# Gated cross-attention block with four rounds of experts: the subtraction of the largest score moved into the exponential

## The reference

```
q   = xn @ Wq.T + bq            # 16 heads of 8 channels
k,v = ctx @ Wkv.T + bkv         # 77 context tokens
att = softmax(q k^T / sqrt(8))  # over the 77 context tokens, per head
x   = x + tanh(g_xattn) * ((att v) @ Wo.T + bo)
x   = x + tanh(g_ffn) * experts(layernorm(x))   # 4 rounds, 4 experts, the 2 best by a router
```

## Time and profile before

| | us |
|---|---|
| median of 3 runs | 538.82 |
| lowest to highest | 538.28 to 539.25 |
| the profiled execution, its own time | 538.98 |
| its span, from the first to the last instruction | 537.2 |

### The profile page before, as it was taken

How to read it: one execution, slowest core, us unless ns; L and a number is a source line. 1 busy time by engine, 2 the same in 40 slices (tenths; PEclk the granted TensorE clock), 3 DMA queues, 4 the chain that set the end, 5 groups by cost and what they waited for, 6 DMA issues and landing times.

```text
span 537.2 us, 8396 instructions
## 1 busy us (share of the span) xinstructions
PE 497.2 (93%) x2529; PEld 402.4 (75%) x2529; DVE 407.7 (76%) x792; ACT 373.1 (69%) x717; POOL 78.7 (15%) x149
## 2 busy tenths in 40 slices
PE   0967998999779999999999999999999999999996
PEld 0945777777567878878888887888788888887884
DVE  3789898889855977697787769768776866876775
ACT  1444556655456887788688778778887877878873
POOL 3374466565300000000000000000000000000000
PEclk9985999999988999999999999999999999999999
DMA  5500000000004012004002100300210040031001
GB/s 135 163 2 0 2 0 0 0 0 0 2 0 159 1 65 94 1 0 159 1 2 83 76 0 1 157 2 0 107 52 1 1 159 0 1 112 67 20 1 39
DMA packets 13063, 22.39 MB, mean 42 GB/s; under 512 B 5200, under 2 KB 9957, under 8 KB 10981
## 3 DMA queue, kind: packets, MB, share of 16 engines
q1 hardware_dynamic: 9648, 21.42, 11.3%
q10 hardware_dynamic: 3381, 0.55, 0.6%
HBM read 20.79 MB, written 1.18 MB: 41 GB/s over the span
## 4 chain that ended last, share of the span: by engine, by line
PE 88%; DVE 6%; ACT 2%; DMA 1%; ACTq 1%; issue 1%; DVEq 0%
PE ps L1121 11%; PE ps L1123 11%; PE ps L1122 11%; PE ps L1101 11%; PE ps L1103 11%; PE ps L1102 11%; PE ps L1015 7%; PE ps L993 4%; PE ps L1002 3%; ACT probT L507 2%; DMA rows_in<-in_L_xattn_bkv_dram 1%; PE ps L949 1%; PE ps L1089 1%; PE ps L1033 1%; DVE v_blk L691 1%
## 5 line engine op out<-in xcount | busy, mean ns | idle before, releaser
L801 DVE TENSOR_TENSOR h_lo<-g_sb,h_hi 128x512 fp32r<-128x512 f32 x256 | 169.8, 687 | 81.2 <-ACT h_hi L597 81.2
L590 ACT ACTIVATE g_sb<-ps,cols 128x512 f32<-128x512 f32 x256 | 175.7, 687 | 75.4 <-PE ps L1103 74.8
L597 ACT ACTIVATE h_hi<-g_sb 128x512 fp32r<-128x512 f32 x256 | 154.1, 631 | 0.0
L1121 PE MATMUL ps<-h_hi,w_hi 128*128 128x512 f32 x256 | 103.5, 404 | 0.0
L1101 PE MATMUL ps<-x_hi,w_hi 128*128 128x512 f32 x256 | 102.2, 399 | 0.8 <-DVE x_lo L795 0.8
L1103 PE MATMUL ps<-x_hi,w_lo 128*128 128x512 f32 x256 | 101.9, 398 | 0.0
L1123 PE MATMUL ps<-h_hi,w_lo 128*128 128x512 f32 x256 | 101.9, 398 | 0.0
L1122 PE MATMUL ps<-h_lo,w_hi 128*128 128x512 f32 x256 | 101.2, 395 | 0.0
L1102 PE MATMUL ps<-x_lo,w_hi 128*128 128x512 f32 x256 | 101.2, 395 | 0.0
L811 DVE SCALAR_TENSOR_TENSOR contrib<-ps,cols,cwb 128x512 f32<-128x512 f32 x64 | 47.8, 746 | 14.0 <-PE ps L1123 8.4
L1101 PEld LDWEIGHTS ps<-x_hi,w_hi 128*128 128x128 f32 x256 | 48.6, 190 | 12.3 <-issue 1.0
(11 more groups left out here) (129 smaller groups left out, 504.1 us busy)
## 6 DMA issues: line engine op xcount, KB each, us to landing
cwb<-cw_rows SPq DMA_DIRECT2D x16, 1024.0 KB, 5.7
x_sb<-in_x_dram SPq DMA_DIRECT2D x4, 256.0 KB, 8.8
w_in<-in_L_ffn_W_dram SPq DMA_DIRECT2D x1, 1024.0 KB, 7.9
out_dram<-xn SPq DMA_DIRECT2D x4, 256.0 KB, 2.3
ctx_sb<-in_ctx_dram ACTq DMA_DIRECT2D x1, 462.0 KB
cw_rows<-cwT SPq DMA_DIRECT2D x8, 16.0 KB, 1.4
wq_in<-in_L_xattn_Wq_dram SPq DMA_DIRECT2D x1, 64.0 KB, 2.7
bv_row<-in_L_xattn_bkv_dram ACTq DMA_DIRECT2D x1, 64.0 KB, 9.1
```

The source lines that it names most:

```text
L590: nc.scalar.activation(g_sb[:, k, :], ps[:, k, :], ACT.Gelu_apprx_tanh, bias=b1_c[:, e * NF + k:e * NF + k + 1]).then_inc(gelu_done, 1)
L597: nc.scalar.activation(h_hi[:, u % 2, k, :], g_sb[:, k, :], ACT.Copy).then_inc(hi_done, 1)
L801: nc.vector.tensor_tensor(h_lo[:, u % 2, k, :], g_sb[:, k, :], h_hi[:, u % 2, k, :].bitcast(F32), ALU.subtract).then_inc(lo_done, 1)
L1121: mm(yb, w2_hi[:, w], hh, start=k == 0, stop=False)
```

## The change

The scores come out of PE negated and scaled: ACT copies Wq's transpose with the factor `-SCALE`, and the bias of q is taken times `-SCALE` too (`bq_s`, a new tile of one column, written by one new ACTIVATE in the start). So the smallest of the negated scores of a head is the negated maximum. DVE takes that minimum (`least`, one tile per parity of b) and subtracts nothing. ACT then computes `exp(-score + least)` straight from PSUM; since the bias is one number per partition and head, this takes one ACTIVATE of 77 columns per head, 8 for each half, in place of one of 616 columns. The tile `shifted` is gone. A score bank may now be written again only once the exponentials have read it: `scores(b+1, half)` waits for `exp_done` of `(b, half)`, and so does the first matmul of the expert stage.

```diff
-        bq_c = cols[:, NCOL - 2:NCOL - 1]
+        bq_s = sb("bq_s", [P, 1])
...
-        mx = sb("mx", [P, H])
+        least = sb("least", [P, 2, H])
...
-        shifted = early("shifted", [P, NQ, HM])
...
-            nc.scalar.activation(wT[:, 0, :], bank(J_W)[:, 0:P], ACT.Copy)
+            nc.scalar.activation(wT[:, 0, :], bank(J_W)[:, 0:P], ACT.Copy, scale=-SCALE)
...
+            nc.scalar.activation(bq_s[:, :], COLS[:, NCOL - 2:NCOL - 1], ACT.Copy, scale=-SCALE)
...
-            def exponentials(b, half, first=False):
-                cols = slice(half * 2 * HM, (half + 1) * 2 * HM)
-                act.wait_ge(sub_done, 2 * b + half + 1)
+            def exponentials(b, s, half, first=False):
+                act.wait_ge(least_done, 2 * b + half + 1)
                 if not first:
                     act.wait_ge(pt_done, NG * b)
                     act.wait_ge(den_done, b)
-                nc.scalar.activation(prob[:, cols], shifted[:, :, :].rearrange("p q n -> p (q n)")[:, cols],
-                                     ACT.Exp, scale=SCALE).then_inc(exp_done, 1)
+                for h in range(2 * HQ * half, 2 * HQ * (half + 1)):
+                    q, k = h // HQ, h % HQ
+                    t = nc.scalar.activation(prob[:, h * M:(h + 1) * M], ps[:, SC + q, k * M:(k + 1) * M],
+                                             ACT.Exp, scale=-1.0, bias=least[:, s, h:h + 1])
+                t.then_inc(exp_done, 1)
...
-                                     ACT.Identity, bias=bq_c[:, 0:1]).then_inc(pre_act, 1)
+                                     ACT.Identity, bias=bq_s[:, 0:1]).then_inc(pre_act, 1)
...
-            def shift(b, half, first=False):
+            def smallest(b, s, half):
 
                 two = slice(2 * half, 2 * half + 2)
                 scores = ps[:, SC + 2 * half:SC + 2 * half + 2, 0:HM].rearrange("p q (h m) -> p q h m", m=M)
                 dve.wait_ge(scores_done, 2 * b + half + 1)
-                nc.vector.tensor_reduce(mx_v[:, two, :], scores, AX.X, ALU.max).then_inc(mx_done, 1)
-                dve.wait_ge(mx_done, 2 * b + half + 1)
-                if not first:
-                    dve.wait_ge(exp_done, 2 * b + half - 1)
-                nc.vector.tensor_tensor(shifted[:, two, :].rearrange("p q (h m) -> p q h m", m=M), scores,
-                                        mx_v[:, two, :].unsqueeze(3).to_broadcast([P, 2, HQ, M]),
-                                        ALU.subtract).then_inc(sub_done, 1)
+                nc.vector.tensor_reduce(least[:, s, :].rearrange("p (q h) -> p q h", q=NQ)[:, two, :], scores, AX.X,
+                                        ALU.min).then_inc(least_done, 1)
...
                 if not first:
-                    pe.wait_ge(sub_done, 2 * b - 1 + half)
+                    pe.wait_ge(exp_done, 2 * b - 1 + half)
...
-            pe.wait_ge(sub_done, 2 * B)
+            pe.wait_ge(exp_done, 2 * B)
```

More of the change, by code:

```diff
@@ L222, in flamingo_gated_block @@
         scores_done = sem("scores_done")
-        mx_done = sem("mx_done")
-        sub_done = sem("sub_done")
+        least_done = sem("least_done")
         exp_done = sem("exp_done")
@@ L551, in attend @@
                 if scores:
-                    exponentials(b + 1, 0)
-                    exponentials(b + 1, 1)
+                    exponentials(b + 1, 1 - s, 0)
+                    exponentials(b + 1, 1 - s, 1)
             assert TC >= 2
@@ L565, in _ @@
             act.wait_ge(moe_ld, 16 * 3)
-            exponentials(0, 0, first=True)
-            exponentials(0, 1, first=True)
+            exponentials(0, 0, 0, first=True)
+            exponentials(0, 0, 1, first=True)
             attend(0, 0, first=True)
@@ L705, in _ @@
                                     ALU.subtract).then_inc(wg_split, 1)
-            mx_v = mx[:, :].rearrange("p (q h) -> p q h", q=NQ)
-            def shift(b, half, first=False):
+            def smallest(b, s, half):
                 two = slice(2 * half, 2 * half + 2)
@@ L747, in attend @@
                 if scores:
-                    shift(b + 1, 0)
+                    smallest(b + 1, 1 - s, 0)
                 if queries:
@@ L753, in attend @@
                 if scores:
-                    shift(b + 1, 1)
+                    smallest(b + 1, 1 - s, 1)
                 if residual:
@@ L761, in _ @@
             dve.wait_ge(xres_step, 2)
-            shift(0, 0, first=True)
-            shift(0, 1, first=True)
+            smallest(0, 0, 0)
+            smallest(0, 0, 1)
             attend(0, 0, values=False, residual=False)
```

## The result

The changed kernel takes 601.84 us (median of 4 runs, 600.19 to 603.5) against 538.55 us: a ratio of 1.1174, 95% interval 1.114 to 1.1208. The forecast was 590.7 us with a range of 568 to 611. The direction and the ring were right; 11 us are missing. The measured time lies in the stretch that the prediction gave to rival C (over 600 us, chance 0.16) and not in that of its own forecast (583 to 600): the clock cost nearly what C said.

What follows compares the result with a forecast made beforehand. PE and DVE were taken as nearly full, PE setting the 5.92 us round. Profiled 538.98 + 36.5 (ring, first and last rounds, start) + 15.4 (clock) = 590.9, median 590.7 us; range 568 to 611.

Steps and rivals of the forecast that it cites:

- the ring: Attention rounds: transposes, moves, widening, eight exponentials, scores, values, transposes close into 8.40 us, from 5.97; +31.6 us over 13 rounds.
- rival C: Attention: clock low for most of each round, recovery late; 606 us at 2.2 us a round, 623 throughout; chance 0.16.
- What bounds the kernel: Attention: PE and DVE nearly full, ACT with room but waiting each iteration for PE's transposes, 29.0 us in all.
- The short exponentials: ACT's 77-column exponentials: 0.33 us each, steps of 0.21, one half 1.80 us, both 3.5 against 1.31 before.
- Rival D: Cheap exponentials at the step's lower end: half 1.05 us, ring 0.75 shorter, 564 us at full clock; chance 0.04.
- The first rounds: Start of attention: first exponentials at about 43.0, later second scores and transposes delay the next scores by 2.7 us.
- The last round: End of attention: `move_rT` behind both halves of the last exponentials delays PE's projection and the attention's end by 2.15 us.
- The sum at the full clock: Whole kernel: 31.6 + 2.7 + 2.15 + 0.1 = +36.5 us; 575.3 us if the clock holds (rival A, chance 0.32).
- The clock: PE's 2.45 us pause each round lowers its clock in most rounds: 1.1 us a round, 15.4 us for 14 rounds.
- The clock behind each wait: Skill's kernel starts each matmul burst cold after a wait; earlier falls agree, but no row showed a pause returning each round.

Runs made afterwards that it cites:

- The run with two buffers: Changed kernel with two buffers for the probabilities, the first half of the exponentials ahead of ACT's moves of the transposed probabilities: 546.64 us.
- the short exponentials alone: Kernel before with 16 exponentials of 77 columns per batch, read from the SBUF copy with a zero bias; subtraction and the scores' wait for it stay: 592.57 us.
- the pause filled: Changed kernel plus 8 unread fp32 matmuls of 128 columns before the first scores of every batch from the third on: 575.11 us.
- the fastest version: Changed kernel with one minimum per query and half, one ACTIVATE per half, two probability buffers and the first half ahead of the moves: 528.62 us.
- its other layout: Kernel before, same instructions, small tiles laid out so the expert stage's tiles lie at the fastest version's addresses: 532.4 us.
- the wait alone: Kernel before with the scores waiting for the exponentials instead of the subtraction; SBUF copy and 616-column exponentials stay: 572.61 us.

## Why the prediction was right, and where it was short

- *What bounds the kernel.* Right: ACT's room could not be used, since its order is tied to PE's transposes. The run with two buffers shows it: the same work in another place of the queue, 546.6 us.
- *The short exponentials.* The step of 0.21 us and the half of 1.80 were measured at 0.21 (3.54 us for 16) and 1.82 to 1.90. Part of that is luck: one operation lasts 0.38 us on the mean, not 0.33, and more than the 0.355 that stood as the upper end, and two of them overlap by 0.17 us, not 0.12. The two errors cancel in the step. Rival D is out.
- *The ring.* 8.40 us worked out, 8.22 measured with the clock held. The ring through the second half and `move_rT` (7.9 us) was not in the prediction as a ring; it was only charged once, for the last round. It didn't change the sum, because it is the shorter one, but it is why the short exponentials alone cost 54 us.
- *The first rounds.* From the first exponentials to exponentials 2 the changed kernel takes 17.85 us (42.05 to 59.90), the one with the pause filled 17.94; 17.7 were worked out (43.0 to 60.7). The length was right. The +2.7 is met only by the latter (60.69 against 57.99); the changed kernel started its first exponentials 0.9 us earlier than forecast, so it is +1.9 there.
- *The last round.* +2.15 worked out; from the start of exponentials 15 to the end of the span the changed kernel takes 405.6 us, before 401.6: +4.0. PE waited 3.54 us for `move_rT` there, and the transposes behind it ran at the low level (2.50 us for ten), which the prediction did not charge.
- *The sum at the full clock.* 575.3 worked out, 575.1 measured with the pause filled. That it is this close is luck: the ring was 0.18 us too long in 13 rounds (2.3 us), and the last round 2 us too short.
- *The clock.* This term was too small: 15.4 us forecast, 26.7 measured, and that is the 11 us by which the forecast missed. The price of one low stretch of 3.4 us (1.43 us) was right, for rounds of 9.76 against 8.22 cost 1.5. Two steps were off: I let part of the low stretch lie in the pause, and it lies behind it, all in work; and I had one low stretch in each round at most, where every third round has two (11.19 us, 3.0 more than 8.22). (2 x 1.55 + 3.0) / 3 = 2.0 us a round, not 1.1. Rival C's price, 2.2 us a round and 606 us, was nearer than the forecast's 1.1. Its reason, a recovery that comes late, holds for every third round; that the level recovers later there is shown, why in every third is not settled.
- *The clock behind each wait.* The kernel of which the Trainium skill tells (TensorE: Matmul & The Clock Gate, HAM oscillation) starts each burst of matmuls cold again after a wait. The trace agrees that the low clock comes back in every round, here with a pause of 2.4 us. It differs in that the bursts don't start cold: the clock is still 1.00 when PE resumes, and falls 0.2 to 1.1 us later in the three rounds looked at above. With the pause filled it stays at 1.00 from 60 to 150.

## What to carry to other kernels

A copy that looks like waste may be what releases a buffer: before folding it away, ask who waits for that buffer, and where the new reader stands in its own queue. An engine with 45% idle time has room only for work that doesn't stand behind the thing it is waiting for; draw every ring through it, not just the first. If a change makes TensorE pause in each round, price the clock by whole low stretches of full work, and test it by filling the pause.

## What was not expected of the hardware

- Where the expert stage's tiles lie in SBUF is worth 1.2% of this kernel: 532.4 against 538.7 us with the same instructions. Between the fastest version and the same kernel with the changed kernel's addresses, means of the 512-column matmuls move by 4 to 5 ns; between the kernel before and its other layout, by 0 to 5. Which tile and which address matter was not tried, nor why.
- Sixteen exponentials of 77 columns queued back to back took 3.54 us from PSUM and 4.08 from SBUF, though one alone lasts longer from PSUM (0.38 against 0.35 us on the mean). The two kernels also differ in the bias (a column for each head, or one column of zeros for all), so that the source is the cause isn't shown.
- PE's clock fell behind pauses of 1.4 us in 5 of 13 rounds (the wait alone), and behind pauses of 2.4 us in all of them (the changed kernel).
